# A convolution stage and a last feed-forward layer reordered in an eight-layer kernel

## The reference

```python
# layer 1: long convolution over channels (L = 512), D = 256 rows in 32 heads of 8
kv = vr[:, :, :, None, :] * x2r[:, :, None, :, :]
y = irfft(rfft(kv, n=2 * L) * k_f)[..., :L] + kv * skip
out = einsum('bhijl,bhil->bhjl', y, x1r)          # x1 = x2 = ctx, v = layernorm(x)
# layer 2 needs mean(|W|) of three 512x2048 matrices before it can round them to -1, 0, 1
# layer 8: feed-forward with the signs of its weights
hidden = relu(einsum('bsd,hd->bsh', x, sign(up_weight)) * up_scale)
out = einsum('bsh,dh->bsd', hidden, sign(down_weight)) * down_scale * output_scale
```

## Time and profile before

| | |
|---|---|
| median of 3 runs | 3387.77 us (3387.43 to 3389.38) |
| profiled execution, its own time | 3388.9 us |
| its span, first to last instruction | 3387.1 us |
| mean granted PE clock | 0.950 of full |
| busy: PE, DVE, ACT, POOL | 86%, 74%, 51%, 27% |
| HBM read, written | 119.03 MB, 4.19 MB |

### The profile page before, as it was taken

One profiled execution on the slowest core, in us unless ns is written; L12 is line 12 of the kernel. 1 busy time (PEld: TensorE's weight loads), 2 busy tenths in 40 slices (PEclk: granted clock), 3 DMA queues, 4 the chain that ended last, 5 costly groups with the idle time before them and its releaser, 6 DMA issues.

```text
span 3387.1 us, 49017 instructions
## 1 busy us (share of the span) xinstructions
PE 2922.5 (86%) x18354; PEld 1703.4 (50%) x18354; DVE 2494.4 (74%) x4562; ACT 1724.4 (51%) x2661; POOL 921.8 (27%) x1361
## 2 busy tenths in 40 slices
PE   7899998892788888768888667999999999988998
PEld 3344666661444444456666433545555455544665
DVE  6787589988766667688888768777777777766333
ACT  3222344444355555179998864444445444454443
POOL 4554000001300000046776774222222222211000
PEclk9999999995999999889999878999999999999999
DMA  6422212121110102100000021000000000021000
GB/s 235 139 91 84 59 55 64 55 63 70 41 32 23 26 17 72 43 31 1 1 1 1 28 92 39 7 1 7 1 7 7 1 7 7 1 72 32 13 19 19
DMA packets 52651, 132.62 MB, mean 39 GB/s; under 512 B 6416, under 2 KB 19536, under 8 KB 51152
## 3 DMA queue, kind: packets, MB, share of 16 engines
q1 hardware_dynamic: 43216, 96.11, 9.0%
q10 hardware_dynamic: 9216, 33.56, 3.3%
HBM read 119.03 MB, written 4.19 MB: 36 GB/s over the span
## 4 chain that ended last, share of the span: by engine, by line
PE 49%; DVE 24%; issue 12%; ACT 9%; POOL 4%; DMA 1%; SPq 0%; DVEq 0%; ACTq 0%; POOLq 0%
PE psum L1263 10%; PE psum L652 6%; PE psum L2231 5%; PE psum L2761 3%; PE psum L2720 3%; ACT area_g L2306 3%; PE psum L823 3%; PE psum L2112 2%; PE psum L2745 2%; PE psum L2730 2%; PE psum L2252 2%; DVE area_a L1870 2%; PE psum L1518 2%; PE psum L1499 2%; DVE xn L3018 1%
## 5 line engine op out<-in xcount | busy, mean ns | idle before, releaser
L2306 ACT ACTIVATE area_g<-area_a 128x2048 bf16<-128x2048 f32 x168 | 334.8, 1997 | 31.4 <-POOL area_a L2175 22.2
L2231 PE MATMUL psum<-area_c,ident_bf 128*128 128x128 bf16 x3328 | 234.2, 236 | 94.1 <-DVE area_c L2340 94.1
L652 PE MATMUL psum<-area_b,area_g 128*128 128x512 f32 x640 | 284.8, 600 | 6.4 <-DVE x_stream L547 3.6
L169 POOL TENSOR_TENSOR rstd<-mean_var,eps_col 128x2 f32<-128x2 f32 x57 | 19.2, 336 | 980.7 <-DVE mean_var L747 497.1
L2231 PEld LDWEIGHTS psum<-area_c,ident_bf 128*128 128x128 bf16 x3328 | 219.1, 107 | 119.9 <-DVE area_c L2340 112.7
L2720 PE MATMUL psum<-area_b,stage 128*128 128x512 f32 (+1 forms) x512 | 237.9, 547 | 0.0
L823 PE MATMUL psum<-xT_high,area_a 128*128 128x256 f16 x1024 | 234.7, 278 | 1.4 <-DVE xT_low L762 1.4
L823 PE MATMUL psum<-xT_low,area_a 128*128 128x256 f16 x1024 | 234.3, 278 | 0.0
L2872 ACT ACTIVATE xn<-psum,small 128x384 f32<-128x384 f32 (+1 forms) x256 | 163.5, 639 | 96.0 <-DVE small L3011 95.8
L3011 DVE TENSOR_REDUCE small<-psum 128x1 f32<-128x384 f32 (+1 forms) x256 | 158.0, 617 | 72.2 <-PE psum L2721 70.4
L2637 POOL TENSOR_TENSOR small<-small,half_pow 128x4 f32<-128x4 f32 x96 | 131.7, 1372 | 273.8 <-DVE small L2958 273.8
(11 more groups left out here) (423 smaller groups left out, 7493.3 us busy)
## 6 DMA issues: line engine op xcount, KB each, us to landing
stage<-in_w ACTq DMA_DIRECT2D x24, 512.0 KB, 4.3
stage<-in_w SPq DMA_DIRECT2D x24, 512.0 KB, 3.7
area_g<-in_toeplitz SPq DMA_DIRECT2D x32, 256.0 KB, 2.6
area_b<-in_ctxT SPq DMA_DIRECT2D x15, 512.0 KB, 3.9
area_b<-area_b SPq DMA_DIRECT2D x24, 256.0 KB, 3.7
stage<-in_ctxT SPq DMA_DIRECT2D x9, 512.0 KB, 3.9
x_stream<-in_x SPq DMA_DIRECT2D x4, 1024.0 KB, 12.2
area_c<-in_ctxT SPq DMA_DIRECT2D x4, 1024.0 KB, 11.2
```

The costliest lines, as they stand in the source:

```text
L652: last = nc.tensor.matmul(psum[:, bank + m, :], toep[:, h % 2, (m - k) * P:(m - k + 1) * P], kv[:, h % 2, k, :], start=(k == 0), stop=(k = ...
L2231: last = nc.tensor.matmul(psum[:, 1, t_ * P:(t_ + 1) * P], identb[:, :], above5[:, t_, c * P:(c + 1) * P], start=(c == 0), stop=(c == KE - 1))
L2306: nc.scalar.activation(junk5[t_], z5[b % 3][:, t_, :], ACT.Sign, bias=fine5[:, par, t_:t_ + 1], scale=-1.0, accum_out=signs5[:, t_:t_ + 1] ...
```

## The change

**Convolution.** (1) GpSimd: `products(h)` stands ahead of the root of step h. (2) The skip matmul uses bank +3 and the turn bank +2 (before: +2 and +3), and PE's waits move with them. (3) TERN0 is 10 instead of 8: the scales are made two steps later; steps 20 and 22 take two chunks. PE's wait for the scales' bank moves to the head of step TERN0 + 1. (4) The context is loaded in halves: positions 0 to 127 at the start, the others in steps 4 to 7, half a MB each; the second table is loaded behind the second tiles of x. (5) ScalarE's four sums of squares come behind the 24 sums of |W|, with their junk output in another place.
**Last layer.** The loops are written out and slices run on: PE's passes of a slice follow those of the one before, the turn comes at group 5 and has two banks; VectorE adds slice b-1 at group 1 of slice b, makes the sums of b+1 at group 2, the norm at 3, the low halves of the turned x at 6. The last slice is stored tile by tile.

```diff
-        TERN0 = 8
+        TERN0 = 10
+        EXTRA0 = (20, 22)
...
+        def chunks0(h):
+            n = h - TERN0 + sum(1 for e in EXTRA0 if e < h)
+            return [] if h < TERN0 else [n, n + 1] if h in EXTRA0 else [n]
...                                                   # sp_stage0
-                sp.dma_start(cT[:, k, :, :], t["ctxT"][:, k]).then_inc(sig("ctxT_loaded"), 16)
-            load_toep(1)
+                sp.dma_start(cT[:, k, :, 0:P], t["ctxT"][:, k, :, 0:P]).then_inc(sig("ctxT_loaded"), 16)
             load_x(1, 0)
             load_x(1, 1)
+            load_toep(1)
...
+                if 4 <= h < 4 + KD:
+                    sp.dma_start(cT[:, h - 4, :, P:S], t["ctxT"][:, h - 4, :, P:S]).then_inc(sig("x_half_loaded"), 16)
...                                                   # pool_stage0
+                products(h)
                 b = front0(h)
                 if b is not None:
                     rstd(slot0(b, 1), 1, slot0(b, 1) + 1, sig("front_rstd"))
-                products(h)
...                                                   # pe_stage0
+                if h == TERN0 + 1:
+                    pe.wait_ge(sig("tables_ready"), 2)
...
-                    pe.wait_ge(sig("y_drained"), h * KD + 3)
-                    nc.tensor.matmul(psum[:, bank + 2, :], skip_mat[:, t_, :], skip_prod[:, h % 2, :], start=True,
+                    pe.wait_ge(sig("y_drained"), h * KD + 4)
+                    nc.tensor.matmul(psum[:, bank + 3, :], skip_mat[:, t_, :], skip_prod[:, h % 2, :], start=True,
...
-                    turn_in(front0(h), 1, bank + 3)
+                    turn_in(front0(h), 1, bank + 2)
...
-                    if m == 2 and skip0(h) is not None:
+                    if m == 3 and skip0(h) is not None:
                         pe.wait_ge(sig("skip_added"), 2 * TT + h)
-                    if m == 3 and front0(h) is not None:
+                    if m == 2 and front0(h) is not None:
                         pe.wait_ge(sig("front_bank_free"), 1 + B + front0(h) + 1)
...                                                   # pe_stage7, after
+            for g in range(B * NJ):
+                b, j = divmod(g, NJ)
+                if j == 0:
+                    pe.wait_ge(sig("front_bank_free"), front7(b, TT, TT + 1))
+                pe.wait_ge(sig("hid_ready"), HID0 + 2 * g + 2)
...
+                if g >= 2:
+                    down(g - 2)
+                if j == 5 and b + 1 < B:
+                    turn_in(b + 1)
...                                                   # dve_stage7, after
+            def y_add(b):
+                for t_ in range(TT):
+                    n = b * TT + t_
+                    xt = X[:, n, :]
+                    dve.wait_ge(sig("down_ready"), TT * B + n + 1)
+                    nc.vector.tensor_tensor(y7[:, t_, :], psum[:, 6 + t_, :], down_scale, ALU.mult).then_inc(sig("ffn0_added"), 1)
+                    dve.wait_ge(sig("ffn0_added"), TT * B + TT + n + 1)
+                    nc.vector.tensor_tensor(xt, xt, y7[:, t_, :], ALU.add).then_inc(sig("skip_added"), 1)
+            for g in range(B * NJ):
+                b, j = divmod(g, NJ)
+                dve.wait_ge(sig("hid_high_ready"), NJ * B + g + 1)
+                nc.vector.tensor_tensor(hTl7[:, 2 * j:2 * j + 2, :], hid7[:, j % 2, :].rearrange("p (m s) -> p m s", m=2),
+                                        hTh7[:, 2 * j:2 * j + 2, :], ALU.subtract).then_inc(sig("hid_low_ready"), 1)
+                if j == 1 and b:
+                    y_add(b - 1)
+                if b + 1 < B:
+                    if j == 2:
+                        x_stats(b + 1)
+                    if j == 3:
+                        x_scale(b + 1)
+                    if j == 6:
+                        x_low(b + 1)
+            y_add(B - 1)
```

More of the change, by code:

```diff
@@ L584, in dve_stage0 @@
                 conv_out(h, 2)
-                if h >= TERN0:
-                    ternary(h)
+                for n in chunks0(h):
+                    ternary(n)
                 if h == HC // 2 + 2:
@@ L681, in act_stage0 @@
                 turned_in(b, 0, b)
+            for h in range(1, B + 1):
+                turned_in(front0(h), 1, 4 * (h % 2) + 2)
+                for n in range(3):
+                    sums(3 * (h - 1) + n)
+            act.wait_ge(sig("x_half_loaded"), 16 * (2 + KD))
             for k in range(KD):
-                if k == 0:
-                    act.wait_ge(sig("ctxT_loaded"), 16 * KD)
                 if k:
@@ L689, in act_stage0 @@
             act.wait_ge(sig("ctx_squares_ready"), KD)
-            for h in range(1, B + 1):
-                turned_in(front0(h), 1, 4 * (h % 2) + 3)
-                for n in range(3):
-                    sums(3 * (h - 1) + n)
             act.wait_ge(sig("tables_ready"), 2)
-            for h in range(TERN0, HC):
-                j, pas, k, c = prep1[1][CHUNKS0 + h - TERN0]
-                n = h - TERN0
+            for n in range(CHUNKS0):
+                j, pas, k, c = prep1[1][CHUNKS0 + n]
                 act.wait_ge(*chunk_loaded(j))
@@ L3208, in down, with turn_in @@
                         last.then_inc(sig("down_ready"), 1)
[L3210 to L3227 removed]
+            def turn_in(b):
+                for t_ in range(TT):
+                    pe.wait_ge(sig("xn_ready"), front7(b, TT, t_ + 1))
+                    pe.wait_ge(sig("front_bank_free"), front7(b, TT, 1))
+                    for k in range(KD):
+                        last = nc.tensor.transpose(psum[:, t_, k * P:(k + 1) * P], xn[:, b % 2, t_, k * P:(k + 1) * P], ident[:, :])
+                    last.then_inc(sig("xT_ready"), 1)
@@ new lines, in pe_stage7 @@
+            for g in range(B * NJ):
[3 more added lines that the diff above has]
+                pe.wait_ge(sig("hid_ready"), HID0 + 2 * g + 2)
+                for m in (2 * j, 2 * j + 1):
+                    out = psum[:, 2 + j % 2, (m % 2) * S:(m % 2 + 1) * S]
+                    for k in range(KD):
+                        for n, xt in enumerate((xTh, xTl)):
+                            last = nc.tensor.matmul(out, w7_up[:, k, m * P:(m + 1) * P], xt[:, b % 2, k, :],
+                                                    start=(k == 0 and n == 0), stop=(k == KD - 1 and n == 1))
+                last.then_inc(sig("up_gate_ready"), 1)
+                if g >= 2:
+                    down(g - 2)
+                if j == 5 and b + 1 < B:
+                    turn_in(b + 1)
```

137 lines of the change are left out of this document (63 added, 74 removed).

## The result

| | before | after |
|---|---|---|
| median of 4 runs | 3387.60 us (3386.98 to 3389.38) | 3338.91 us (3337.96 to 3340.69) |
| ratio, 95% interval | | 0.9855 [0.9843, 0.9868] |
| span of the profiled execution | 3387.1 us | 3336.4 us |
| mean granted PE clock | 0.950 | 0.951 |

The change is 48.7 us faster; 3341.0 was predicted, within 3334 to 3353. In the profiled executions the spans differ by 50.7 us.

The account below looks back on a forecast made before the run. PE, busy 86% of the span, was taken as the bound, so only its waits and low clock could yield time. Convolution 22.9 plus last layer 23.9 gave 46.8 off 3388.9: 3342.1, median 3341; range 3334 to 3353, 3336 to 3346 at 0.60.

Parts of the forecast that it names:

- Steps 1 to 8: Convolution: with products ahead of the root, PE becomes the bound and a step takes 10.03 instead of 11.24; 8.5 us.
- The start: Before step 1: half the context's bytes let products start at 20.5, PE at 21.65 with the clock holding; 3.8 us gained.
- Sums two steps later: Convolution: step 8 becomes an ordinary step, 8.5 us gained; a remaining PE stall at step 10 costs 2.3.
- Banks: Convolution steps 9 to 16: swapped banks remove PE's wait for the gate addition, 8 x 0.55 = 4.4 us.
- The loads: Convolution steps 4 to 7: moved context loads priced at nothing, at up to 1.2 us in each step.
- VectorE beside the products: Steps 1 to 8: VectorE slowed by GpSimd's products, 9.3 busy of 10.03, not the bound; possibly 0.7 more.
- Convolution: Whole convolution: 3.8 + 8.5 + 8.5 + 2.1 = 22.9 us gained.
- The last layer: Last layer: 24.7 from PE's two waits per slice, less 1.4 for late additions, plus 0.6 at the end; 23.9 us.
- The rival of code that comes in too slowly: Last layer: PE's written-out program arrives too slowly; at 35 ns more for each instruction, 3397 us; chance 0.03.
- rival with the clock in the convolution: VectorE or the clock keeps part: steps 1 to 8 3.8, start 1.1, behind step 10 about 2; 3348; chance 0.16.

Follow-up runs that it names:

- e1: The kernel before with one edit, GpSimd's products ahead of the root of a convolution step; 3380.15 us, ratio 0.9983.
- e3: The changed kernel with GpSimd's root ahead of the products again, all else as after; 3351.15 us, ratio 0.9893.
- e2: The kernel before with only the last layer as in the changed kernel; 3363.61 us, ratio 0.9928.
- e10: The changed kernel with half of VectorE's weight sums a step early, plus twelve throwaway TensorE matmuls in step 10; 3346.49 us, ratio 0.9872.
- e11: The changed kernel with half of VectorE's weight sums a step early, plus four throwaway TensorE matmuls in step 10; 3341.08 us, ratio 0.9855.
- e4: The changed kernel with the weight sums prepared at step 8 again instead of step 10; 3346.39 us, ratio 0.9875.
- e9: The changed kernel with three throwaway TensorE matmuls just ahead of the sums' matmuls of step 10; 3341.90 us, ratio 0.9857.
- e6: The changed kernel with the skip product's and the turn's psum banks swapped back, products still first; 3347.05 us, ratio 0.9878.
- e7: The changed kernel with its last layer written out but in the old order of work inside a slice; 3363.16 us, ratio 0.9931.
- e5: The changed kernel with the context's columns loaded whole before the first step, as before; 3343.51 us, ratio 0.9865.
- e12: The changed kernel once more, word for word; 3340.18 us, ratio 0.9853.
- e8: The changed kernel with the first half of VectorE's weight sums (L297, L301) moved to the end of step 9; 3338.76 us, ratio 0.9853.

## Why the prediction was right, and where it was not

*Steps 1 to 8*, 8.5 predicted: pitch 9.88 instead of 10.03, 9.4 us from step 1 to step 8 (step 1 took 9.99). That the queue alone held the products is shown (e1, e3). That the bound behind it is PE is shown for the swapped banks, where no wait is left; with the old ones 0.26 of the pitch hangs on the gate addition. The 0.15 are the seams that I had added (0.05) and the skip matmul: I took 0.96 from a row where PE had waited just before it, and it takes 0.86. The time of the passes, 8.58, was right.

*The start*, 3.8 predicted: 4.75. Products at 19.79, not 20.5: I took the end of ScalarE's copies, 20.45, from the one execution of before, and it varies (19.62 in e2, whose code there is the same). The clock held behind an idle time of 2.10 us, as chosen, but by luck as much as by reason: e10 and e11, whose code is the same up to there, lost it after 2.04 and 2.05.

*Sums two steps later*, 8.5 less a 2.3 at step 10: the stall at step 8 went entirely, 18.53 - 9.88 = 8.65; with all else as after it would be 7.5 (e4, 17.34 - 9.88), and 0.9 more in step 9. The cost at step 10 was 14.23 - 9.44 = 4.8, double. The stall itself was nearly right: VectorE's copy ended 6.1 us behind the skip matmul, 5.5 were predicted, so PE stood 2.63, not 2.1; 0.44 of that is the copy itself, slow beside GpSimd (below). The step that failed is the clock: I had it hold behind 2.1 us and put its fall into a rival at about 2; e9 measured 1.7.

*Banks*, 4.4 predicted for steps 9 to 16: 0.70 a step, 5.6 in all. e1 and e6 put it on the banks alone.

*The loads*, priced at nothing: no wait of PE in steps 4 to 7, right. Small pieces did move slower at the start (below): the last half landed at 18.61, not near 15, still before ScalarE's last copy.

*VectorE beside the products*: 9.3 busy in a step predicted, 9.38 measured, with PE never waiting for it; the further 0.7 that the prediction allowed for did not come.

*Convolution*: 22.9 predicted, 23.6 measured. The total is near by offsets: the loss at step 10 was put 2.5 too low, and every gain was put too low as well.

*The last layer*, 24.7 - 1.4 + 0.6: the stage is 229.16 long, 228.6 + 1.4 predicted, and no wait of PE is left, so the additions cost at most 0.6, not 1.4; behind the last pass 1.15 instead of 0.6 were won. The rival of code that comes in too slowly is out (e7: 0.2 us the other way, PE busy all of 229.16).

*The untouched stages*: 0 in the prediction, 1.9 measured, and that is the largest thing it left out. Steps 16 to 31 and these stages took 2922.4 to 2928.2 us in the 14 profiled executions, and 2.9 apart in before and e2 with one code; so it is not shown that the 1.9 come from the change at all. The prediction's rival with the clock in the convolution did not reach there. So the total came within 0.1% partly by luck: 1.9 and, the 2.5 at step 10 taken off, 0.7 were won on top, and of the terms that I had feared only the clock's fall behind step 10 cost anything.

What stays open: which places make up a middle, and whether it hangs on what ran before or on the execution. Two places were read (1120 and 1320 us), in one pair; the losses of e5 and e4 were not traced one by one. Nor is the least value known: after and e11 have 2922.7 and 2922.4, and e1, the 0.7 of its step 16 taken off, 2922.0.

## What to carry to other kernels

Ask of a wait what stands behind it in the same queue: here a GpSimd queue in the wrong order cost 1.1 us a step, and the bank that a result lands in mattered in those steps only once that was mended. Undo each part by itself, since e3 and e1 say together what neither says alone. And below 0.2% read a change where it was made: one code took 2.9 us more or less in stages that nobody touched, so a small gain or loss need not show in the total, and a total that agrees to 0.1% does not show that the sum was right.

## What the runs showed of the hardware

*The clock.* Behind stands of about the same length it fell or held: 1.85, 2.10 and 2.15 (held; the last is the start of e3, e4 and e6 to e9), 2.42 (held), 2.04 and 2.05 (fell, start of e10 and e11), 2.63 (fell in after, e3, e6, e7 and e12, held in e5), 2.73, 3.27 and 3.67 (fell). Behind the restart at 1120 us the pieces were at full speed again after 3.5 us in after and not yet after 4.5 in e8. So the length of the stand alone does not decide; what else does is not shown. Work in the stand held the clock (e9). The Trainium skill (TensorE: Matmul & The Clock Gate, Part 1) says that the activity is watched by a free-running window, so that the same code pays differently from run to run. No run here shows the window. That the same code pays differently the traces do show: e8, e10 and e11 have one code up to step 9, and the clock held at the start of the first and fell in the others. e12, whose middle repeated after's to 0.1 us, shows that it need not.

*VectorE beside GpSimd.* A copy of 128x3 (L301) took 0.61 us in step 10 and 0.17 in e8, where it stands at the end of step 9 with GpSimd idle. In step 10 it ends with GpSimd's skip product (123.47 + 1.26 = 124.73, the copy 124.75). All fourteen traces are alike: in seven it stands beside the skip product, takes 0.61 and ends within 0.03 us of it, in seven it stands alone and takes 0.17.

```profile
123.47 1.26 POOL L491 TENSOR_TENSOR area_g<-area_a,area_g 128x512 f32<-128x512 f32 x1
```
```profile
116.86 0.17 DVE L304 COPY partial_sums<-scalars 128x3 f32<-128x3 f32 x1
```

By the Trainium skill (SBUF — State Buffer, Who interferes with whom) the shared port is an exclusive lock; a copy that ends when the neighbour ends agrees.

*Pieces of 512 bytes.* The same three microseconds of the start, with the context in halves (after) and whole (e5); the last two columns are DMA share and GB/s:

```profile
14.00:17.00 3.00, 3.00 (x16) 3.00 (x15) 2.44 (x6) 1.80 (x3) 0.00 (x0) 1.00 1.19 298
```
```profile
14.00:17.00 3.00, 3.00 (x16) 3.00 (x15) 2.56 (x6) 1.79 (x3) 0.00 (x0) 1.00 1.01 429
```

298 GB/s at a share of 1.19 against 429 at 1.01; in both only the context is moving then. The pieces of the halves also leave gaps between them in SBUF, which no run tells apart from their size. The Trainium skill (DMA: Bandwidth & Descriptors, Specifications) puts full rate at 512 bytes and more; this trace disagrees, at 0.7 of the rate. The halves paid all the same, since they are half the bytes.
